# Expert rows counted in units of 64 (blocks of 256, 384 and 320), and a hinted back edge on the tensor engine's loop over expert pairs

## What is computed

```python
gate = jnp.einsum('bsd,ed->bse', x, Wg) + routing_bias
_, top_idx = jax.lax.top_k(gate, K)                   # K = 4 of E = 8 experts
mask = jax.nn.one_hot(top_idx, E, dtype=gate.dtype).sum(-2)
masked_gate = jnp.where(mask > 0, gate, -jnp.inf)
weights = jax.nn.softmax(masked_gate, axis=-1) * mask
out = _swiglu(x, Ws1, Ws2, Ws3)                       # the shared part
h1 = jnp.einsum('bsd,ehd->ebsh', x, W1)
h2 = jnp.einsum('bsd,ehd->ebsh', x, W2)
eo = jnp.einsum('ebsh,edh->ebsd', jax.nn.sigmoid(h1) * h1 * h2, W3)
out = out + jnp.einsum('ebsd,bse->bsd', eo, weights)
```

## Time and profile before

| what | value |
| --- | --- |
| median of 3 runs | 996.76 us (995.49 to 996.99) |
| the profiled execution | 993.37 us, its span 991.6 us |
| TensorE clock granted | 0.998 of full speed |
| PE busy | 972.4 us, 98% of the span |
| ACT, DVE, POOL busy | 508.9, 559.6, 544.6 us |
| chain that ended last | PE 83%, POOL 6%, DVE 4%, DMA 3%, issue 3% |

### The profile page before, as it was taken

The page is one execution under the profiler, slowest core; times in us unless marked ns, Lnnn a source line. Parts: engine busy times, 40 slices in busy tenths (PEclk is TensorE's granted clock), DMA queues, the critical chain, the costliest instruction groups (busy, mean ns, idle before and its releaser), DMA issues.

```text
span 991.6 us, 25401 instructions
## 1 busy us (share of the span) xinstructions
PE 972.4 (98%) x8054; PEld 799.8 (81%) x8054; DVE 559.6 (56%) x1411; ACT 508.9 (51%) x1250; POOL 544.6 (55%) x513
## 2 busy tenths in 40 slices
PE   9998999999999999999999999999999999999997
PEld 4665666788887888888788878788888887887886
DVE  4998687745544455545444545454455454544686
ACT  3676354455554555555444545445455554554366
POOL 4554027766733347623955016076888880885873
PEclk9999999999999999999999999999999999999999
DMA  6959024355542333353245214228764882795785
GB/s 229 248 139 184 1 55 131 94 161 146 166 114 78 104 92 97 98 173 95 61 144 145 49 48 128 54 50 190 127 98 75 127 124 53 109 131 87 101 146 144
DMA packets 168051, 113.86 MB, mean 115 GB/s; under 512 B 113596, under 2 KB 160191, under 8 KB 166848
## 3 DMA queue, kind: packets, MB, share of 16 engines
q0 software_dynamic: 29808, 58.37, 27.5%
q1 hardware_dynamic: 115888, 33.15, 16.4%
q10 hardware_dynamic: 22304, 21.76, 6.6%
HBM read 47.09 MB, written 43.12 MB: 91 GB/s over the span
## 4 chain that ended last, share of the span: by engine, by line
PE 83%; POOL 6%; DVE 4%; DMA 3%; issue 3%; ACT 1%; SPq 1%; POOLq 0%; ACTq 0%; DVEq 0%
PE psA L1072 51%; PE psB L1103 21%; PE psA L1020 5%; POOL y_sum L758 3%; DMA rows_by_place<-y_rows,place 2%; POOL rows_by_place L694 2%; PE psB L1106 1%; PE psC L1054 1%; PE psA L1103 1%; DMA y_sum<-rows_by_place,place 1%; PE psB L1033 1%; PE psC L1047 1%; PE psC L1174 0%; SPq L518 0%; DVE g_lo L1504 0%
## 5 line engine op out<-in xcount | busy, mean ns | idle before, releaser
L873 ACT ACTIVATE sil<-psA 128x256 f32<-128x256 f32 (+1 forms) x456 | 178.8, 399 | 283.6 <-PE psA L1072 259.1
L758 POOL DMA_INDIRECT y_sum<-rows_by_place,place x128 | 199.7, 1560 | 82.8 <-issue 38.0
L1494 DVE SCALAR_TENSOR_TENSOR g<-psA,sil 128x256 f32<-128x256 f32 (+1 forms) x160 | 72.0, 450 | 306.5 <-ACT sil L873 306.3
L1072 PE MATMUL psA<-xb_odd,work 128*128 128x256 f16 x1980 | 221.1, 273 | 0.5 <-issue 0.5
L1072 PEld LDWEIGHTS psA<-xb_odd,work 128*128 128x128 f16 x1980 | 193.2, 98 | 24.1 <-issue 1.5
L1103 PE MATMUL psB<-work,g_hi 128*128 128x256 f16 x1260 | 211.1, 273 | 0.0
L1072 PE MATMUL psA<-xb,work 128*128 128x256 f16 x1782 | 199.0, 273 | 2.2 <-issue 1.1
L1072 PEld LDWEIGHTS psA<-xb,work 128*128 128x128 f16 x1782 | 173.8, 98 | 23.9 <-issue 3.8
L1494 DVE SCALAR_TENSOR_TENSOR psC<-psA,sil 128x256 f32<-128x256 f32 (+3 forms) x296 | 133.1, 450 | 77.6 <-ACT sil L873 71.2
L1103 PE MATMUL psB<-work,g_lo 128*128 128x256 f16 x630 | 171.7, 273 | 0.0
L705 POOL DMA_INDIRECT rows_by_place<-y_rows,place x96 | 95.2, 992 | 135.1 <-DMA rows_by_place<-y_rows,place 121.3
(11 more groups left out here) (176 smaller groups left out, 1033.3 us busy)
## 6 DMA issues: line engine op xcount, KB each, us to landing
stage<-wpack POOLq DMA_DIRECT2D x9, 2176.0 KB, 8.9
rows_by_place<-eb ACTq DMA_DIRECT2D x57, 256.0 KB
work<-xT SPq DMA_DIRECT2D x7, 512.0 KB, 6.0
work<-half_beta SPq DMA_DIRECT2D x6, 512.0 KB, 4.8
work<-x_tok POOLq DMA_DIRECT2D x6, 512.0 KB, 6.5
rows_by_place<-eb ACTq DMA_DIRECT2D x6, 384.0 KB
rows_by_place<-zeros SPq DMA_DIRECT2D x1, 2112.0 KB, 13.2
rows_by_place<-y_rows,place POOLq DMA_INDIRECT x128, 2.5
```

The source lines that it names most:

```text
L758: pool.indirect_dma_start(out=y_sum[:, n, :], out_offset=None, in_=xs, in_offset=bass.IndirectOffsetOnAxis(ap=place[:, k, n:n + 1], axis=0 ...
L873: act.activation(sil[r0:r0 + n, c % SLOTS, 0:T], psA[0:n, chunk_bank(c, T), 0:T], ACT.Silu, scale=1.0 / (XS * WS)).then_inc(silu_ready, 1)
L1072: last = pe.matmul(dst, W[:, ws, k, ci, :], xb[slot][:, KD * xs_ + k, 0:T], start=(k == 0 and n == 0), stop=(k == KD - 1 and n == 2))
L1494: dve.scalar_tensor_tensor(gated_rows(g, c, 0, n, T), src, 1.0 / (XS * WS), sil[r0:r0 + n, c % SLOTS, 0:T], ALU.mult, ALU.mult).then_inc(g ...
```

## The change

Rows are counted in units of 64. An expert now gets blocks of 256, at most one of 384 (`wide`) and at most one of 320 (`short`, `TM`). With U units, the last two bits say which of the two tails there are, and each tail takes 4 units more out of the blocks of 256; an expert with under 12 units gets blocks of 256 alone, which occurs for none here. `down`, the loads, and the stores still go by groups of 128, so a block of 320 moves three groups. One more group of zeros is written behind each expert.

| expert | rows | blocks before | blocks after |
| --- | --- | --- | --- |
| 0 | 2834 | 10 x 256, 384 | 10 x 256, 320 |
| 1 | 3068 | 12 x 256 | 12 x 256 |
| 2 | 1038 | 3 x 256, 384 | 3 x 256, 320 |
| 3 | 2143 | 7 x 256, 384 | 7 x 256, 384 |
| 4 | 1319 | 4 x 256, 384 | 4 x 256, 320 |
| 5 | 1455 | 6 x 256 | 3 x 256, 384, 320 |
| 6 | 2934 | 10 x 256, 384 | 10 x 256, 384 |
| 7 | 1593 | 5 x 256, 384 | 5 x 256, 320 |

The test for zero blocks of 256 ahead of the inner loop goes, and a test for the block of 320 comes behind the one for 384, on every engine. The pair loop of PE starts at slot 0 of a block in which instructions are fetched, and its first instruction is a hint that names its closing jump.

```diff
+UNIT = P // 2
+TM = TL - UNIT
...
         def expert_blocks(eng, w, row, run):
-            full, odd, first, group = row
+            (full, wide, short), first, group = row
...
-            with eng.If(full > 0):
-                with eng.Fori(0, turns) as i:
...
-            with eng.If(odd > 0):
+            with eng.If(wide > 0):
                 run(TL, eng.snap(first + full), None if group is None else eng.snap(group + JB * full), 4 + w)
+            with eng.If(short > 0):
+                run(TM, eng.snap(eng.snap(first + full) + wide),
+                    None if group is None else eng.snap(eng.snap(group + JB * full) + JL * wide), 5 - w)
...
-                J = T // P
+                J = -(-T // P)
...
             def expert_turns(w, beside):
-                with pe.If_lt(first_of[w][pe.engine], past_of[w][pe.engine]):
...
-                with pe.If_ne(odd_of[w][pe.engine], 0):
+                with pe.If_ne(wide_of[w][pe.engine], 0):
                     past = pe.snap(past_of[w], donate=True, min_val=SA, max_val=SA + NR)
                     ffn_block(w, past, TL, 4 + w, beside=beside)
+                with pe.If_ne(short_of[w][pe.engine], 0):
+                    past = pe.snap(past_of[w], donate=True, min_val=SA, max_val=SA + NR)
+                    wide = pe.snap(wide_of[w], donate=True, min_val=0, max_val=1)
+                    ffn_block(w, pe.snap(past + wide), TM, 5 - w, beside=beside)
...
-            with pe.Fori(0, E // 2) as p:
+            with nc.Fori(0, E // 2, engines=[pe.engine], hint_back_edge=True, head_slot={pe.engine: 0}) as p:
...
-                t.add(dve.tensor_scalar(cnt_i[:, 0, :], inc[:, :, NT - 1], 1.0, P - 1.0, ALU.mult, ALU.add))
+                t.add(dve.tensor_scalar(cnt_i[:, 0, :], inc[:, :, NT - 1], 1.0, 2.0 * P - 1.0, ALU.mult, ALU.add))
...
-                t.add(dve.scalar_tensor_tensor(pad[:, :, :], tail.unsqueeze(2).to_broadcast([P, E, JB]), 1.0 - P,
+                t.add(dve.scalar_tensor_tensor(pad[:, :, :], tail.unsqueeze(2).to_broadcast([P, E, JB]), 1.0 - 2 * P,
```

More of the change, by code:

```diff
@@ L92, in build @@
     assert NT < FIELD and NR < FIELD and (NG + 1) * FIELD ** 2 < 1 << 24
+    MAIN = TB // UNIT
+    LEAST = 3 * MAIN
+    assert MAIN == 4 and TL == 6 * UNIT and TM == 5 * UNIT and N // UNIT < FIELD
     OWN = [[], [0, 1], [2], [3], [4], [5], [6]]
@@ L378, in pair_rows @@
                 return [expert_row(eng, 2 * p + w) for w in range(2)]
-            word = eng.value_load(pairs[0:1, bass.ds(p, 1)], min_val=1, max_val=(NT + 1) * FIELD ** 2 - 1)
+            word = eng.value_load(pairs[0:1, bass.ds(p, 1)], min_val=1, max_val=(N // UNIT + 1) * FIELD ** 2 - 1)
             first = eng.snap(word & (FIELD - 1), min_val=0, max_val=NR)
-            n = [eng.snap((word >> FIELD_BITS) & (FIELD - 1), min_val=1, max_val=NT),
-                 eng.snap(word >> (2 * FIELD_BITS), min_val=1, max_val=NT)]
-            return [(eng.snap(n[0] >> 1), eng.snap(n[0] & 1), first, None),
-                    (eng.snap(n[1] >> 1), eng.snap(n[1] & 1), eng.snap(first + ((n[0] + 1) >> 1)), None)]
+            n = [eng.snap((word >> FIELD_BITS) & (FIELD - 1), min_val=MAIN, max_val=N // UNIT),
+                 eng.snap(word >> (2 * FIELD_BITS), min_val=MAIN, max_val=N // UNIT)]
+            rows = [units_of(eng, u) for u in n]
+            full, wide, short = rows[0]
+            return [(rows[0], first, None),
+                    (rows[1], eng.snap(eng.snap(eng.snap(first + full) + wide) + short), None)]
         def early_slot(i):
@@ L400, in rows_from @@
                 return None if group is None else group + JB * n
[L402 to L408 removed]
+            with eng.Fori(0, turns) as i:
+                run(TB, first + 2 * i, rows_from(2 * i), 2 * w)
+                left = eng.snap(full - 2 * i)
+                with eng.If(left > 1):
+                    run(TB, first + (2 * i + 1), rows_from(2 * i + 1), 2 * w + 1)
+            with eng.If(wide > 0):
                 run(TL, eng.snap(first + full), None if group is None else eng.snap(group + JB * full), 4 + w)
+            with eng.If(short > 0):
+                run(TM, eng.snap(eng.snap(first + full) + wide),
+                    None if group is None else eng.snap(eng.snap(group + JB * full) + JL * wide), 5 - w)
         def blocks_until(eng, e):
[L413 to L414 removed]
+            (full, wide, short), first, _ = expert_row(eng, e)
+            return eng.snap(eng.snap(eng.snap(first + full) + wide) + short)
         FINISH = [[S1 + q for q in OWN[i]] + list(range(sum(EXTRA[:i]), sum(EXTRA[:i + 1]))) for i in range(S2)]
@@ L1098, in down @@
                         pe.wait_ge(high_doubled, g + 1)
-                    for j in range(T // P):
+                    for j in range(-(-T // P)):
                         o = down_sum(j)
@@ L1118, in _ @@
             pair_words = [row_regs(f"pair_word{p}") for p in range(E // 2)]
-            groups_of = [row_regs(f"groups{w}") for w in range(2)]
+            units_in = [row_regs(f"units{w}") for w in range(2)]
             first_of = [row_regs(f"first_block{w}") for w in range(2)]
             past_of = [row_regs(f"past_full{w}") for w in range(2)]
-            odd_of = [row_regs(f"odd_block{w}") for w in range(2)]
+            wide_of = [row_regs(f"wide_block{w}") for w in range(2)]
+            short_of = [row_regs(f"short_block{w}") for w in range(2)]
             late_of = row_regs("late_block")
@@ L1158, in expert_turns @@
             def expert_turns(w, beside):
-                with pe.If_lt(first_of[w][pe.engine], past_of[w][pe.engine]):
-                    first = pe.snap(first_of[w], donate=True, min_val=SA, max_val=SA + NR)
-                    past = pe.snap(past_of[w], donate=True, min_val=SA, max_val=SA + NR)
-                    with pe.Fori(first, past, 2) as g:
-                        ffn_block(w, g, TB, 2 * w, beside=beside)
-                        odd = pe.snap(g + 1)
-                        with pe.If(odd < past):
-                            ffn_block(w, odd, TB, 2 * w + 1, beside=beside)
@@ L1168, in expert_turns @@
-                with pe.If_ne(odd_of[w][pe.engine], 0):
+                first = pe.snap(first_of[w], min_val=SA, max_val=SA + NR)
+                past = pe.snap(past_of[w], min_val=SA, max_val=SA + NR)
+                with pe.Fori(first, past, 2) as g:
+                    ffn_block(w, g, TB, 2 * w, beside=beside)
+                    odd = pe.snap(g + 1)
+                    with pe.If(odd < past):
+                        ffn_block(w, odd, TB, 2 * w + 1, beside=beside)
+                with pe.If_ne(wide_of[w][pe.engine], 0):
@@ L1210, in read_sizes @@
                     pe.wait_ge(blocks_ready, 1)
[L1211 removed]
+                    for regs in (first_of[1], past_of[1], wide_of[1], short_of[1]):
                         nc.regs_mov(regs, SA)
```

86 lines of the change are left out of this document (54 added, 32 removed).

## The result

The changed kernel takes 1002.41 us (median of 5 runs, 999.85 to 1005.07), against 995.49 us for the kernel before (5 runs, 994.08 to 996.99): ratio 1.0076, 95% interval 1.0060 to 1.0091. It is slower by about 7 us; forecast were 992.6 us, in 987.2 to 996.8. The profiled execution took 999.85 us, 6.5 us more than the one in the earlier trace rows, and so did its span.

The account below looks back on a forecast made before the run. The prediction took PE, alone through the experts, to bound the kernel, then POOL's gathers behind them. Its terms, 3.5 + 1.9 - 0.35 - 0.3 - 0.6, summed to 4.15 us saved: 992.6 us, in 987.2 to 996.8.

Parts of the forecast that it names:

- Tails of 320: Experts 0, 2, 4 and 7: a 320 tail replaces a 384 one, 0.88 us saved each, 3.5 us together.
- X: Lateness of ACT's silu in a 320 block, from one taken jump and three register instructions: 0.38 us, between 0 and 1.25.
- Expert 5: Three blocks of 256 and tails of 384 and 320 replace six blocks: 63.7 us for 65.60, 1.9 us saved.
- Expert 1's end: Expert 1 has neither tail; a second skipped test, less the test ahead of the loop, loses 0.35 us (0 to 0.9).
- instruction fetches: PE's longer pair loop, with expert 1's jumps and the loop's turns: 0.6 us lost, from 0 to 5.6.
- over 25 packets: Sign for the third rival: more than 25 packets on the fetch queue, with PE idle over 1 us beside them.
- The hint itself gains nothing over before: At the pair loop's turns the hint saves nothing, since turns behind a tail are hidden anyhow.
- The third rival: PE's pair loop no longer stays on chip, each pass fetches anew: slower, 1007 us, chance 0.09.
- Registers beside `up` [...] cost nothing: Two or three more register instructions in a block lie under PE's matmuls and cost nothing.
- Start: Ahead of the first expert block, pad rows queued before POOL's scatter can delay it: 0.3 us lost.

Follow-up runs that it names:

- one_skip_act: one_skip, with the tail's numbers put into registers of ACT ahead of each expert's loop; ratio to the kernel before 1.0020.
- hint_only: The kernel before with only the hint and the slot on PE's pair loop; ratio 0.9999.
- plain_loop: The changed kernel with PE's pair loop opened as before, without hint and slot; ratio to the kernel before 1.0219.
- cut pair: Kernel before and changed kernel, each with POOL's weight conversions cut to 8 columns a piece for experts 2 to 7; 992.90 and 996.46 us.
- dead_0: hint_only plus a never-run body of 60 matmuls behind the odd experts' tail, loop head at slot 0; ratio to the kernel before 1.0004.
- dead_100: dead_0 with the loop's head at slot 100 of a block, no instruction differing; ratio to the kernel before 1.0039.
- head_184: The changed kernel with the head of PE's pair loop at slot 184 of a block instead of slot 0; ratio to the kernel before 1.0062.
- one_skip: The changed kernel with one PE jump over both tails where an expert has none; ratio to the kernel before 1.0074.

## Why the prediction was wrong

The step that failed first is the price of the open jump at expert 1's end: the prediction took it as the time of one packet, 1.4 us at most, with a small share, and the runs show 3.65 us of waiting and then a stretch at the lower clock. The second is the wait of DVE for POOL, which it put at nothing. From the 4.15 us saved that it summed to the 6.5 us lost, 10.7 us are to be explained: 4.0 at expert 1's end, 3.6 in blocks of 256, 2.6 in expert 5, 0.9 in the tails of 384, 0.8 at the start and 0.2 in the tails of 320, less 1.4 after the experts.

- **Tails of 320 (3.5 us): right.** 3.3 us, chunk 2 at 4.24, 4.50, 4.09 and 4.34 us, released by DVE, as in the earlier trace rows. Only expert 2's, at 4.50 us and 15.46 in all, left the forecast span. The mechanism, ACT's lateness, was shown by one_skip_act.
- **Tails of 384 (not in the sum): missed.** The prediction charged X to the tails of 320 alone. In the trace the test for the wide tail is now four instructions of ACT in place of two, with a pause of 0.3 us between them, ahead of a first silu that was already late: +0.57 and +0.34 us.
- **Expert 5 (1.9 us saved): wrong, -0.7.** The blocks came as counted, and with POOL's work cut the expert took 63.77 us. In the changed kernel its wide tail's load took 11.80 us, PE waited 1.2 us for it, and DVE was held in its first block, which took 12.31 us. The prediction took the loads of that expert as in time.
- **Expert 1's end (0.35) and instruction fetches (0.6): the largest miss, 5.0 us for 0.95.** The prediction named the place, "the second perhaps onto code just asked for", and gave an upper bound of 5.6 us for it and the turns. It priced an open fetch by the time of its packet, 1.4 us; measured, such a jump at this place takes 3.6 to 4.7 us, and the lower clock behind it costs 1.3 us more here, and up to 2.9 in other kernels. And it gave the case a small share of the term, where the places of the instructions in the built program settle it: expert 1's inner loop ended in block 5, the second test stood in block 6, and its landing place in block 7. The sign that the prediction named, over 25 packets, did not come: there were 22, and one of them cost 5 us.
- **"The hint itself gains nothing over before": right over before (hint_only), wrong for the changed loop,** where it saves 15 us. The third rival, "the loop no longer stays on chip", was real, and it is the hint that kept it off: plain_loop came to 1017.75 us, where the rival said 1007.
- **"Registers beside `up` [...] cost nothing": nothing contradicts it.** Plain blocks are 10.70 us in both. But the blocks of 256 that are not plain cost 3.6 us more, in the rows looked at through DVE behind POOL. The prediction had no term for two engines that hold each other up. The cut pair puts some 4 us of the difference on POOL's conversions, expert 5's included, and does not tell DVE's holds from the transfers.
- **Start (0.3): 1.06 us.** Pads, scatter and a 427 ns jump onto the slot. hint_only, which has the jump alone, starts its experts 0.24 us later than the kernel before; the rest was not tested alone.

The Trainium skill (Runtime: NRT & Kernel Launch, Instruction fetch mechanics) has a taken branch stall when its target lies outside a window of two pages of 256 instructions. The prediction set that aside. dead_0 and dead_100 agree with it for code on its first pass (227 against 3740 ns). For code that has run it does not hold: in dead_0 the closing jump of a loop of six such blocks took 0.23 us three times and caused no fetch, and in the kernel before, without any hint, it took 0.22 to 0.24 us, with one packet in 336:913 us. For DVE and POOL the Trainium skill (SBUF — State Buffer, SBUF: two separate sides) has an exclusive lock: who starts first keeps the shared ports for the whole instruction. The row at 600.13 agrees, 1.68 us for 0.43. The row at 403.77 agrees only in part: DVE's record begins 0.7 us ahead of POOL's subtraction and still ends behind it, as if DVE had waited out the scatter's issue and then the subtraction too, 2.65 us in all.

## What to carry to other kernels

Count where the instructions lie before adding a branch body to a loop: a jump over code that has never run took 0.23 to 0.38 us when it landed in the block of 256 in which PE had been at work or in the next, and 3.6 to 4.7 us beyond it, and then 1.3 to 2.9 us more in clock. Count from the block in which PE had been at work, not from one that it has only just entered. A loop that grows past what stays on chip needed the hint for its closing jump, and a second hint undid it. And when a tuned engine gets something to do 0.5 us earlier or later, look at what DVE reads from SBUF beside POOL's long steps: cutting POOL's steps was worth 2 us in one of these kernels and 6 in the other.

## What the runs showed of the hardware

- A jump to instructions not fetched: 3.6 to 5.1 us. In the changed kernel it came with one packet of 16 KB that itself takes 1.07 us. The packet's time is not the price.
- A loop of 1349 instructions (matmuls counted as two) was not fetched again without a hint; one of 1847 was, 32 packets for 6 in 700 us, and was not with one. With two hints the packets came back (49 in all, against 22).
- After 4.59 us of idleness PE's granted clock was at 0.50 for 2.7 us in the changed kernel, and at 1.00 again after. After 4.63 and 4.84 us in head_184 and one_skip it lasted for 5.9 and 5.5 us.
- DVE's product from two SBUF operands (0.43 us alone) waits out a POOL `tensor_tensor` of 1.5 us and ends 0.3 us behind it, 1.68 us in all; with one operand in PSUM it stays at or under 0.43 us.
